# An attention stage that takes heads in pairs: causal masking moved between TensorE, VectorE and GpSimd

## What is computed

```python
B, S, D, H, E, F = (2, 128, 128, 16, 16, 512)
HEAD = D // H
...
        b, s, _ = hidden_states.shape
...
        x = layer_norm(hidden_states, ln1_w, ln1_b)
        q = (x @ q_w + q_b) / math.sqrt(HEAD)
        k = x @ k_w + k_b
        v = x @ v_w + v_b
        split = lambda t: t.reshape(b, s, H, HEAD).transpose(0, 2, 1, 3)
        q, k, v = (split(q), split(k), split(v))
        scores = jnp.einsum('bhqd,bhkd->bhqk', q, k)
        causal = jnp.tril(jnp.ones((s, s), bool))
        scores = jnp.where(causal, scores, neg)
        attn = jax.nn.softmax(scores, axis=-1)
        ctx = jnp.einsum('bhqk,bhkd->bhqd', attn, v)
```

## Time and profile before

| | us |
|---|---|
| median of 3 runs (2671.39 to 2681.03) | 2673.97 |
| the profiled execution | 2672.96 |
| its span, first to last instruction | 2671.2 |
| attention stage, first block (unit 0, steps, last pass B) | 120.7 to 686 |
| attention stage, third block | 1749.8 to 2317 |

### The profile page before, as it was taken

How to read it: one execution, slowest core, us unless ns; L and a number is a source line. 1 busy time by engine, 2 the same in 40 slices (tenths; PEclk the granted TensorE clock), 3 DMA queues, 4 the chain that set the end, 5 groups by cost and what they waited for, 6 DMA issues and landing times. The chain is left out here.

```text
span 2671.2 us, 45728 instructions
## 1 busy us (share of the span) xinstructions
PE 1847.3 (69%) x10834; PEld 1034.2 (39%) x10928; DVE 1659.7 (62%) x5110; ACT 949.1 (36%) x1988; POOL 944.6 (35%) x1548
## 2 busy tenths in 40 slices
PE   3499889899710981499990075479998899840693
PEld 2133333333510770289980043223333333330472
DVE  7488778787350224867764485688887788451223
ACT  2256556566400330100000032336665566510231
POOL 4022222222445440068770563012222222337342
PEclk8689999999755995689995588679999999855797
DMA  3501111110002435000003001301011110001344
GB/s 84 212 14 26 27 27 26 25 24 6 1 25 68 124 113 146 0 0 0 0 4 36 16 16 47 106 25 26 26 25 27 27 26 14 1 4 51 109 135 128
DMA packets 109183, 120.08 MB, mean 45 GB/s; under 512 B 31264, under 2 KB 71584, under 8 KB 107936
## 3 DMA queue, kind: packets, MB, share of 16 engines
q1 hardware_dynamic: 92448, 96.50, 13.8%
q0 software_dynamic: 8192, 16.86, 1.9%
q10 hardware_dynamic: 8320, 4.19, 0.6%
HBM read 71.01 MB, written 45.71 MB: 44 GB/s over the span
## 5 line engine op out<-in xcount | busy, mean ns | idle before, releaser
L733 DVE CUSTOM_DVE_ANT_0 pA<-pA,causal 128x512 f32<-128x512 f32 (+3 forms) x1536 | 823.9, 582 | 183.0 <-PE pA L576 172.7
L777 ACT ACTIVATE wt<-pB 128x512 f32<-128x512 f32 (+3 forms) x1536 | 654.3, 496 | 442.2 <-PE pB L617 290.2
L818 POOL TENSOR_SCALAR_AFFINE_SELECT wt<-wt 128x128 f32<-128x128 f32 x1024 | 290.7, 293 | 767.6 <-ACT wt L777 746.3
L576 PE MATMUL pA<-ka,qa 125*128 125x512 bf16 (+3 forms) x1536 | 486.7, 343 | 71.1 <-PEq L272 30.0
L617 PE MATMUL pB<-qa,ka 128*128 128x512 bf16 (+3 forms) x1442 | 428.6, 333 | 51.9 <-issue 23.8
L633 PE MATMUL pC<-wt,va 128*32 128x512 f32 (+3 forms) x3072 | 347.5, 499 | 0.0
L617 PEld LDWEIGHTS pB<-qa,ka 128*128 128x128 bf16 x1536 | 145.2, 97 | 420.5 <-ACT wt L777 256.9
L576 PEld LDWEIGHTS pA<-ka,qa 125*128 125x128 bf16 x1536 | 147.5, 98 | 248.7 <-DVE mx L733 164.5
L733 DVE DVE_READ_ACCUMULATOR2_ANT mx<- 128x1 f32 x1536 | 217.0, 141 | 0.0
L1209 POOL DMA_INDIRECT y<-eo,dest x128 | 122.5, 957 | 185.3 <-issue 112.4
L1071 POOL DMA_INDIRECT xin<-keep_v,keep_send x128 | 126.9, 992 | 82.6 <-DVE keep_send L1044 43.8
(11 more groups left out here) (236 smaller groups left out, 2430.5 us busy)
## 6 DMA issues: line engine op xcount, KB each, us to landing
w<-in_L_ffn_fc_w_dram SPq DMA_DIRECT2D x64, 256.0 KB, 2.8
qa<-qk_parts SPq DMA_DIRECT2D x192, 64.0 KB
ka<-qk_parts SPq DMA_DIRECT2D x192, 64.0 KB
xi<-xin SPq DMA_DIRECT2D x32, 258.0 KB, 3.6
qk_parts<-qp SPq DMA_DIRECT2D x24, 256.0 KB, 2.4
qk_parts<-kp SPq DMA_DIRECT2D x24, 256.0 KB, 2.8
xin<-zero SPq DMA_DIRECT2D x4, 1032.0 KB, 7.1
y<-zero SPq DMA_DIRECT2D x4, 1024.0 KB, 13.1
```

What stands on the lines that cost most here:

```text
L576: pe.matmul(slot(s, n)[:, 0:b - a], qa[s.stage][0:MROW, h, i * P:(i + 1) * P], ka[s.stage][0:MROW, h, a:b], start=True, stop=True).then_in ...
L733: vec.tensor_tensor_reduce(out=slot(s, n)[:, 0:size], in0=slot(s, n)[:, 0:size], in1=mask, scale=1.0, scalar=LOWEST, op0=ALU.add, op1=ALU.max,
L777: act.activation(wt[g % NW][h][:, 0:e - a], pB[(g * GH + h) % NB][:, 0:e - a], ACT.Exp).then_inc(exp_done, 1)
L818: pool.affine_select(out=block_, in_=block_, compare_op=ALU.is_ge, fill=0.0, base=0, pattern=[[1, P]], channel_multiplier=-1).then_inc(mas ...
```

## The change

- **Layout.** `qa` and `ka` hold two heads in one column block: the even head on partitions 0 to 63, the odd one on 64 to 127 (`HROW` = 64), so they are half as wide. `load_qk` issues two DMAs where it issued one.
- **Pass A.** A piece is two matmuls, one for each head of a pair, over 48 rows each, into the two banks of a slot; there are two slots (four banks) for three banks before. `PIECE` has 24 entries for 48. Where a piece touches the diagonal, four more matmuls add the mask in PSUM: `pick_lo` and `pick_hi` select 64 rows each of the constants `future_lo` and `future_hi`. DVE takes a plain maximum over both heads in one operation. The float32 constant `causal` goes.
- **Splits.** The splitting of maxima moves from DVE to POOL, in two chains of four operations: after the mask of group 1 (low half) and after that of group 8 (high half). DVE keeps the maximum of both halves, `top`.
- **Pass B.** Scores go in pairs, over 51 rows each. `wt` holds four heads in one tile, and POOL masks all four with one operation once all four exponentials are there. `pC` shrinks from two banks to one.
- **Order.** The products of the last two groups of a unit move into the first two groups of the next step. MAX_HI stays at the same place of the list, which with 24 pieces is two pieces ahead of the end. SP loads unit u + 2 once the scores of unit u − 1 are done.

```diff
@@ constants @@
+            for name, upper, lower in (("lo", -HROW, 0), ("hi", 0, HROW)):
+                pick, future = c["pick_" + name], c["future_" + name]
+                for rows, base in ((slice(0, P), upper), (slice(0, HROW), lower)):
+                    chain.link(pool.memset(pick[rows, :], 0.0))
+                    chain.link(pool.memset(future[rows, :], 0.0))
+                    chain.link(pool.affine_select(out=pick[rows, :], in_=pick[rows, :], compare_op=ALU.not_equal, fill=1.0,
+                                                  base=base, pattern=[[-1, P]], channel_multiplier=1))
+                    chain.link(pool.affine_select(out=future[rows, :], in_=future[rows, :], compare_op=ALU.is_ge,
+                                                  fill=LOWEST, base=base, pattern=[[-1, P]], channel_multiplier=1))
@@ load_qk @@
-            sp.dma_start(dst[r * HD:(r + 1) * HD, :, :],
-                         w["qk_parts"][which, split[r], bass.ds(u, 1)]
-                         .rearrange("o (h d) t -> (o d) h t", d=HD)).then_inc(a["qk_loaded"][stage], 16)
+            for side in range(2):
+                at = side * HROW + r * HD
+                sp.dma_start(dst[at:at + HD, :, :],
+                             w["qk_parts"][which, split[r], bass.ds(u, 1)]
+                             .rearrange("o (p s d) t -> s (o d) p t", s=2, d=HD)[side]).then_inc(a["qk_loaded"][stage], 16)
@@ ffn_attention @@
+    PAIRS = GH // 2
+    PIECE = [(p, i, a, min(a + HALF, (i + 1) * P)) for tiles in (range(HT, BT), range(HT))
+             for i in tiles for a in range(0, (i + 1) * P, HALF) for p in range(PAIRS)]
         order.insert(LATE + 6, MAX_HI)
         if contexts:
-            order[12:12] = [CTX_HI, CTX_LO]
+            order[8:8] = [CTX_HI, CTX_LO]
-    NA, NB = 3, 3
+    NA, NB = 2, 3
-        pA = [ps(f"pA{i}", [P, HALF]) for i in range(NA)]
+        pA = [ps(f"pA{i}", [P, 2, HALF]) for i in range(NA)]
-        pC = ps("pC", [P, SEQ])
+        pC = ps("pC", [P, HALF])
@@ SP: step @@
-                        sp.wait_ge(pv_done, s.u * NCH)
+                        sp.wait_ge(st_done, s.u * NCH)
@@ PE: piece @@
+                    diagonal = b == (i + 1) * P
+                    out = slot(s, n)
+                    for q in range(2):
+                        rows = side(q, KROWS)
+                        last = pe.matmul(out[:, q, 0:b - a], qa[s.stage][rows, p, i * P:(i + 1) * P],
+                                         ka[s.stage][rows, p, a:b], start=True, stop=not diagonal)
+                    if diagonal:
+                        for part, skip in (("lo", 0), ("hi", HROW)):
+                            for q in range(2):
+                                rows = side(q, HROW)
+                                last = pe.matmul(out[:, q, b - a - P + skip:b - a], c["pick_" + part][rows, :],
+                                                 c["future_" + part][rows, skip:], start=False, stop=part == "hi")
+                    last.then_inc(a_done, 1)
@@ PE: scores @@
+                    reached(pe, exp_done, v.u * NCH + (g * GH + 2 * p + 1 - (NB - 1)))
+                    for h in (2 * p, 2 * p + 1):
+                        rows = side(h, KROWS + 3)
+                        pe.matmul(pB[(g * GH + h) % NB][:, 0:e - a], ka[v.stage][rows, p, j * P:(j + 1) * P],
+                                  qa[v.stage][rows, p, a:e], start=True, stop=True).then_inc(st_done, 1)
@@ PE: products @@
                         if DIAG[g]:
-                            pe.wait_ge(masked, v.u * NDIAG + (GH * sum(DIAG[:g]) + h + 1))
+                            pe.wait_ge(masked, v.u * NDIAG + (sum(DIAG[:g]) + 1))
@@ PE: step @@
                         if g >= LAG:
-                            products(s, g - LAG)
+                            products(s.shift(-1), g - LAG)
+                        elif not fixed(s, 1):
+                            products(s.shift(-2), NG + g - LAG)
@@ DVE: step @@
-                            vec.tensor_tensor_reduce(out=slot(s, n)[:, 0:size], in0=slot(s, n)[:, 0:size], in1=mask,
-                                                     scale=1.0, scalar=LOWEST, op0=ALU.add, op1=ALU.max,
-                                                     accum_out=mx[a // HALF][:, i, h:h + 1]).then_inc(a_used, 1)
+                            vec.reduce_max(mx[a // HALF][:, i, 2 * p:2 * p + 2], slot(s, n)[:, :, 0:b - a],
+                                           AX).then_inc(a_used, 1)
@@ ACT: weights @@
-                        if g == 1 and not fixed(s, 1):
+                        if g == LAG - 1 and not fixed(s, 1):
+                            copy_low(s)
-                        if g == LATE_G + LAG:
+                        if g == LATE_G + LAG - 1:
@@ POOL: step @@
+                        if DIAG[g]:
+                            apart(pool, exp_done, v.u * NCH + (g * GH + GH))
+                            block_ = wt[g % NW][:, :, 0:P]
                             pool.affine_select(out=block_, in_=block_, compare_op=ALU.is_ge, fill=0.0, base=0,
-                                               pattern=[[1, P]], channel_multiplier=-1).then_inc(masked, 1)
+                                               pattern=[[0, GH], [1, P]], channel_multiplier=-1).then_inc(masked, 1)
+                        if g == SPLIT_LO:
+                            split_low(s)
+                        if g == SPLIT_HI and more:
+                            split_high(s)
```

More of the change, by code:

```diff
@@ L516, in ffn_attention, with side @@
                                                         sem("pv_done"), sem("cT_ready"))
-        dve = sem("dve_a")
+        dve, split_link = sem("dve_a"), sem("split_link")
+        top_ready = sem("top_ready")
+        def side(h, rows):
+            return slice((h % 2) * HROW, (h % 2) * HROW + rows)
         def fixed(s, upto):
@@ L752, in last @@
+                            if e == LATE:
+                                late = slice(HT, BT)
+                                vec.wait_ge(a_used, event(s, n))
+                                vec.tensor_tensor(top[:, late, :], mx[0][:, late, :], mx[1][:, late, :],
+                                                  ALU.max).then_inc(top_ready, 1)
                 def last(s):
-                    vec.wait_ge(a_used, before(s))
-                    for k in range(4):
-                        split(s, 0, k, k)
@@ L768, in copy_context, with copy_low @@
                     at = half * HALF
-                    act.copy(cT[:, at:at + HALF], pC[:, at:at + HALF]).then_inc(cT_ready, 1)
+                    act.copy(cT[:, at:at + HALF], pC[:, :]).then_inc(cT_ready, 1)
+                def copy_low(s):
+                    act.wait_ge(pv_done, s.u * NCH - NCH)
+                    if not fixed(s, 2):
+                        act.wait_ge(a_done, before(s) - (NEV - ORDER[2].index(CTX_LO) - 1))
+                    copy_context(0)
                 def weights(s):
@@ L806, in stage, with split, split_high, split_low @@
                                      .rearrange("p (t h r) -> p t h r", t=BT, h=GH)).then_inc(v_staged[s.stage], 1)
+                def split(s, half, links):
+                    t = slice(half * HT, (half + 1) * HT)
+                    src = top if half else mx[0]
+                    parts = [mparts[:, t, :, r] for r in range(3)]
+                    pool.tensor_copy(parts[0], src[:, t, :]).then_inc(split_link, 1)
+                    apart(pool, split_link, links + 1)
+                    pool.tensor_tensor(rest[:, t, :], src[:, t, :], parts[0], ALU.subtract).then_inc(split_link, 1)
+                    apart(pool, split_link, links + 2)
+                    pool.tensor_copy(parts[1], rest[:, t, :]).then_inc(split_link, 1)
+                    apart(pool, split_link, links + 3)
+                    pool.tensor_tensor(parts[2], rest[:, t, :], parts[1], ALU.subtract).then_inc(mparts_ready, 1)
+                def split_high(s):
+                    apart(pool, top_ready, s.u + 1)
+                    split(s, 1, s.u * (LINKS_LO + LINKS_HI))
+                def split_low(s):
+                    apart(pool, a_used, before(s))
+                    split(s, 0, s.u * (LINKS_LO + LINKS_HI) - LINKS_LO)
                 def first(s):
```

168 lines of the change are left out of this document (59 added, 109 removed).

## The result

The changed kernel takes 2,781.65 us (median of 4 runs, 2,779.36 to 2,790.26) against 2,674.06 us (4 runs) before: a ratio of 1.0404, interval 1.0374 to 1.0434. It is 4% slower where I had forecast 2,555 us and a gain. The profiled execution took 2,790.26 us (span 2,788.5, against 2,671.2).

What follows compares the result with a forecast made beforehand. DVE and PE both needed some 28.3 us of a 33.7 us step, the rest being waits. Gains of 70 (plain steps), 47 (loop turns) and 3 (first units), less 4 (loads), took 116 us off 2,672.96: 2,555 us, range 2,475 to 2,640.

Steps and rivals of the forecast that it cites:

- the maximum: DVE, per step: plain reductions over both heads of a pair take 21.0 us instead of 24.6.
- the first rival: PE, pieces and scores: row pairs don't run side by side, so 39.8 us a step and 2,835 us; chance 0.10.
- 28.0 to 24.0 start to start: PE, per step: its work, timed from start to start of operations, falls from 28.0 to 24.0 us.
- The mask matmuls: PE, 16 diagonal pieces of a step: four added matmuls each cost 3.4 us in all, bounds 1.3 and 6.4.
- The mask of four heads: POOL, pass B: one affine_select for four heads costs 1.1 us against 4 × 0.29, saving no POOL time.
- PE's wait at the boundary: Step's end, hand-over of the maxima: 2.5 us of standstill on each plain step, bounds 0 and 4.
- The loads: Loads of q and k rows: hidden in the steps, 2 us more each time in the projection stage, −4 in the sum.
- The waits inside the step are now 5.4 ... I take 4.0: Plain step: waits between engines fall from 5.4 to 4.0 us, giving a step of 30.5 us.
- With the granted clock at 1.0 outside loop turns: PE at a step's first score: waits 2 to 3 us for the maxima's DMA while the clock stays at 1.0.
- the rival that cools PE: Step boundary: a 4 us wait plus 1.8 us of slow clock gives back 73 us, 2,628 us; chance 0.15.
- the last passes B: The two last passes B, led by ACT and untouched by the change: 0 us gained.
- The first units: The two first units, DVE-bound, less the longer hand-over: 2 × 1.6 = 3 us gained.

Runs made afterwards that it cites:

- e1_early: The changed kernel with MAX_HI, the hand-over of the upper maxima, three pieces earlier in the list: 2,686.43 us, ratio 1.0041 to the kernel before.
- e15_early_nomask: e1_early with the mask matmuls of pass A left out, so maxima include future keys of the diagonal block: 2,721.47 us, 1.0132.
- e4_mask: The kernel before with only the four heads' exponentials in one tile, masked by one affine_select on GpSimd: 2,656.78 us, 0.994.
- e17: e1_early with the products of the group two back placed between the two score pairs instead of behind the second: 2,714.17 us, 1.0145.
- e20: e1_early with each row maximum taken over only the first 128 keys of a piece (work left out): 2,590.45 us, 0.9651.
- e22: e1_early with each exponential taking only the first half of its columns (work left out): 2,624.49 us, 0.9803.
- e2_warm: The changed kernel with eight dummy matmuls ahead of the wait for the maxima at each step's start: 2,755.96 us, 1.0322.
- e13_mask_split: The kernel before with one mask for four heads and the splits of the maxima, both on GpSimd: 2,642.31 us, 0.9862.

## Why the prediction was wrong, by its steps

Most terms of the sum came out. Of the plain step I had forecast DVE 23.5 us and it is 24.0; ACT 21.3, and it is 21.9. (By its own terms the maximum should have stood at 22.7 − 16 × 0.08 = 21.4 instead of 21.0; and 4.1 + 4.1 + 3.4, which the first rival multiplies, is 11.6 and not 11.4. Neither moves the forecast much.) PE gained more than forecast: by busy time it fell from 31.5 to 24.5 (e1_early at full clock), by 7.0, where I had 28.0 to 24.0 start to start, by 4.0. Reductions of 1,024 elements take 1.22 us, as those from SBUF in the earlier trace rows. Row pairs run side by side: the next piece starts 0.23 us after a pair of scores, against 0.21 for single matmuls; the first rival is out. The mask matmuls cost some 1.1 us a step by e15_early_nomask, under my lower bound of 1.3 and not the 3.4 that I took. The mask of four heads takes 0.63 us where I had 1.1: by the earlier trace rows I had priced columns, and e4_mask gains 17 us from what I had called no saving. POOL has 4.3 us less of it a step (32 × 0.293 against 8 × 0.634). PE's wait at the boundary is 54.6 us in 28 waits, 2.0 each, forecast 2.5. The loads cost nothing that shows.

Two steps failed, both of them judgements on waiting:

**"The waits inside the step are now 5.4 ... I take 4.0".** By busy time PE was idle 2.3 us of a step at full clock before (33.8 − 31.5; the earlier trace rows) and 7.8 us in e1_early, where the boundary costs nothing (32.35 − 24.5). The change took 7.0 us of work from PE and gave 1.4 us of time. Without the boundary's 2.5 my forecast stood at 28.0, the measured step at 32.4: 4.4 us × 30 = 132 us of the error. In the forecast's own terms, its 24.0 us of PE's work subtracted, the 4.0 of waiting became 8.4. I had reasoned that two slots of a pair hold more DVE work than three banks and so waits would shrink with the work. Of the 56.0 us that DVE waited for pieces, which I put down to groups of products, 11 were three turns of the loop. What the table of waits shows is that PE's single stream is handed from one wait to another: for a bank that ACT hasn't read, then for a slot that DVE hasn't. PE's weight loads waited 71 us for ACT in 342 us before and 118 in e1_early. e17 moved these waits, e20 and e22 each took a part away. Before, PE's busy time (31.5 of 33.7) left little room for such waits; that they were there and hidden is my reading.

**"With the granted clock at 1.0 outside loop turns".** This step belongs to the rival that cools PE, to which I gave 0.15. Its cause was right and its size wrong. I had priced a wait of 4 us and 1.8 us of cold; the wait is 2.0, and the half clock that follows lasts 10 us, with a second stretch of 7 us in some steps that begins at small diagonal pieces. The clock in the steps averages 0.83. Against e2_warm's 34.5 us at full clock that is about 3.4 us a step once the turns are set apart, 102 us of the error, and 17 us more in the last passes B, which I had put at zero. I had taken the price of a cold stretch from the earlier trace rows, where the queue behind it was full of work for PE. With 8 us of idle time in a step it took 10 us here until the clock was back, and 13.6 behind a turn in e1_early, against 3.4 before; that the idle time is the reason is argued and not shown.

Together: 132 + 102 + 17 = 251, less about 12 for the boundary and 15 outside the stages (11 us shorter, where I had 4 longer for the loads), so 224 of the 235 by which the profiled execution missed. The first units, 3 us by my forecast, gave nothing; 8 us stay without a term. The two main terms are not independent: e15_early_nomask has less work on PE and a lower clock, and e20_early_short_max has the same work, less idle time in the step (6.3 us for 7.8 at full clock) and a higher clock. Both fit waits inside the step bringing the clock down.

The Trainium skill (TensorE: Matmul & The Clock Gate, "A second HAM failure mode: psum-queue depth-cycling") describes a kernel in which PE idles briefly between groups of matmuls while it goes round its PSUM banks, often enough that the clock swings between its two levels. By that rule, the second stretch at half clock (393 to nearly 400 us, with no wait above 0.81 us ahead of it) is what this change should have been suspected of; I had weighed only the long wait. The trace agrees with it as far as the stretches go, but these short waits alone don't decide it. In e1_early's step at full clock the same small pieces stand behind waits of 0.36 and 0.81 us (at 561.73 and 562.86), and the clock stays at 1.00. What tips it in one step and not in the other is open.

So is the change itself slow, or only its place for MAX_HI? With the hand-over three pieces earlier it is 0.4% slower than the kernel before (at most 0.8% by the interval). Its gain is lost to the clock: its full-clock steps of 32.4 us are 1.4 us shorter than before, its mean step of 35.7 us is 0.9 longer. The two parts that leave PE's order alone (mask and splits on GpSimd, e13_mask_split) beat both kernels by 1.4 and 5%.

## What to carry to other kernels

When a change takes work from the engine that was busiest, redo the waits, not only the work: here 7.0 us less of PE gave 1.4, since one in-order stream now waited in turn for two others. Place a hand-over by the time that its DMA needs, not by its index in a list, for here three places in the order were worth 95 us. Where TensorE's idle time in a loop grows, price the granted clock over whole steps (here a step at 0.86 took 4.0 us longer than one at 1.00), and prefer the parts of a change that leave its stream dense.

## What was unexpected of the hardware

- The granted clock dropped to 0.50 for 10 us some 2.4 us after a 1.78 us wait had ended, and for 7 us more in the same step behind gaps below 1 us (369 to 379 and 393 to 400 of the changed kernel). Nearly the same gaps in e1_early left it at 1.00.
- Behind PE's wait at a turn of the loop (3.5 us before, 3.2 in e1_early) the clock was 0.50 for 3.4 us before the change and for 13.6 in e1_early.
- Less work on TensorE did not make the kernel faster: 64 matmuls a step left out gave 2,721 us for 2,686, at a clock of 0.80 against 0.88 (e15_early_nomask), and with less work on VectorE and the same on TensorE the clock was 0.94 (e20_early_short_max).
- One affine_select over four blocks of 128 columns takes 634 ns, four single ones 4 × 293, yet 384 columns in one block of the earlier trace rows took 868.
- Of the four mask matmuls of a diagonal piece the second pair starts 0.05 us behind the first (390.41 and 390.46 in the changed kernel), though I had given the four 0.21 us.
